# A decay projection in two waves, and the last block's inverse split between GpSimd and VectorE, in a linear-attention and expert kernel

## The chip, the cores and the metric

The kernel runs on one core of one Trainium2 chip. The metric is the device time of one execution in microseconds.

## The reference

One layer in float32 over x of 8 sequences, 512 steps, 256 channels (16 heads of 16). The first half mixes each step with the one before, makes r, k, v, a decay w, a removal direction kk with a strength a, and runs a state of 16x16 per head through the steps:

```python
w2 = jnp.tanh(xwa @ decay_w1.T) @ decay_w2
w = -jax.nn.softplus(-(time_decay + w2)) - 0.5
kk = k + jnp.tanh(xk @ kkk_w1.T) @ kkk_w2        # then divided by its norm per head
a = jax.nn.sigmoid(time_aaaaa + xwa @ aaa_w1.T @ aaa_w2)
...
def step(s, inp):
    q_, w_, k_, v_, a_, b_ = inp                 # w_ = exp(-exp(w)), a_ = kk, b_ = -kk * a
    sa = jnp.einsum('bhij,bhj->bhi', s, a_)
    s = s * w_[:, :, None, :] + sa[..., None] * b_[:, :, None, :] + v_[..., None] * k_[:, :, None, :]
    return (s, jnp.einsum('bhij,bhj->bhi', s, q_))
```

The outputs are normed per head, a bonus of r, k and v is added, and they are gated, projected by Wo, added to x and layer-normed. The second half sends each of the 4,096 tokens to one of 8 experts (the largest of 8 logits), norms it, and applies W1 (256 to 1,024), relu, W2 (back to 256), the residual and a last layer norm.

## The kernel before, in words

The 512 steps are cut in 16 blocks of 32 (`TB`). Within a block the recurrence is solved as a triangular system: `scores` makes the products of keys, removals and reads for all pairs of steps of a head; the part of it that belongs to removals is a 32x32 matrix for each of the 128 pairs of sequence and head, and its inverse is made on GpSimd (`invert`), one matrix per partition, column by column: for s from 30 down to 1 a product of s rows and 31-s columns (L1911) and its addition (L1914), 60 dependent operations. The scores go there over HBM by SP (`scores_to_pairs`: four stores to scr_n at L478, one load of `Up` at L483) and the inverse comes back the same way (`inverse_to_heads`: store to scr_u at L491, tokens of x at L460, four loads at L502). PE then multiplies by it (`solve`, in two parts, L718).

The blocks are staggered over the passes of one loop, `body(n)`, n from -2 to 18, written out for each engine in program order. In body n the projections and scores are those of block n+1, keys and values of block n are turned, block n-1 is solved, read out and its state updated, block n-2 is gated and projected by Wo, and block n-3 has its router logits taken. Nothing is scheduled by a planner: the order of calls in each engine's `body` is the order of its queue.

PE's results lie in six PSUM banks that a `Ring` gives out in a fixed order. An entry such as `k@3` means bank 3; a job may start once the reader of the job before it in the same bank has run (`freed` says which step that is), and `wait_empty` waits for that. In the stretch around the change PE runs `hidden` (L610), `gates`, `square` for k (both L576), the turn of some keys (L670), then `decay_a_kk` and `ma_mk` through `from_hidden` (L622: z with all 128 rows of the hidden vector, then a beside kk and ma beside mk, each with 32 rows), `router` and `project_out` (L576), `solve` part one (L718), `norms` (L576), `solve` part two, `square` for r and v, turns, `read_out` (L752), `bonus` (L576), `update` (L740) and `scores` (L662).

ScalarE (from `keep_z`) takes z with its bias, its sigma into the bank (L1058), a, ma, the absolute value (L1064), the logits of block n-3 (L1212), the square of kk (L1097), then after a table load (L1035) the logarithm (L1117), the norms (L1121), and the decays. VectorE, after the mixing for the next blocks, adds k to kk in `sum_kk` (L1420), runs the scan over sigma (L1400) in `sum_decays`, `key_gain` (L1406, L1408), `add_tokens` of block n-2 (L1546), which frees the bank that `norms` takes, `gain_keys` (L1424), the token statistics, `key_exponent` (L1412, L1414), `keep_x` (L1511), `normed_kk` (L1461), `decay_reads` (L1452), `decay_kk` (L1483), `removal` (L1467), `decay_keys` (L1429), `bonus_terms` (L1434), `mask_removal` (L1476) and `mask_keys` (L1445), for which `scores` waits. All these lines record operations for 128 partitions of 512 columns.

The last block is 15 (`last`). When its scores are done, no projections are left to fill the time of its inverse. W2 (8 MB, one DMA of 1 MB per expert, L513) is loaded over the arrays of the loop by `load_experts`, the first four experts in body 15 and the others in body 16.

## Time and profile before

| | |
|---|---|
| median of 3 runs | 1071.95 us (1068.2 to 1084.34) |
| profiled execution | 1076.19 us, span of its instructions 1074.1 us, mean granted TensorE clock 0.951 |
| PE / DVE / ACT / POOL busy | 980.1 / 768.0 / 519.9 / 613.1 us |
| blocks' loop | to about 660 us of the span |
| last inverse and routing | about 660 to 767 us |
| experts | 767 to 1,064 us |

Times within the span count from its start. The page names engines PE (TensorE), DVE (VectorE), ACT (ScalarE), POOL (GpSimd) and SP (SyncE). A row of the timeline merges instructions of the same kind that follow each other. Matmul times are modelled at their ends, so their sums run a little over the time that they take.

### The profile page before, as it was taken

How to read it: one execution, taken by the hardware profiler on the slowest of the kernel's cores; microseconds unless marked ns; L12 is line 12 of the kernel's file. 1: busy time of each engine (PE TensorE's matmuls, PEld its weight loads, DVE VectorE, ACT ScalarE, POOL GpSimd, SP SyncE). 2: the span in 40 equal slices, each digit the busy share in tenths (PEclk: the TensorE clock that was granted, in tenths of full speed). 3: DMA queues.
4: the chain of work that ended last, by engine and by line, in shares of the span. 5: the costliest groups of instructions: out<-in, count | busy, mean ns of one | idle time of the engine just before them, and what ended most of it. 6: DMA issues, size and time to landing. Idle time of an engine off the chain costs nothing.

```text
span 1074.1 us, 42156 instructions
## 1 busy us (share of the span) xinstructions
PE 980.1 (91%) x16652; PEld 801.8 (75%) x16653; DVE 768.0 (71%) x1793; ACT 519.9 (48%) x1081; POOL 613.1 (57%) x1135
## 2 busy tenths in 40 slices
PE   8898989999999989999999998679899999999995
PEld 5676777777777767777777776557899898989894
DVE  5766788889879778887688885266476666666663
ACT  4474576677677576676476783221122121212120
POOL 1088786788886787785867876810133333333321
PEclk9997999999999999998799998689999999999998
DMA  5113225225324225224143133746545445544430
GB/s 121 40 21 81 71 33 110 65 51 111 77 47 101 70 44 111 72 42 107 17 101 87 28 91 85 206 115 232 217 163 176 161 174 162 176 158 170 158 119 4
DMA packets 208894, 112.14 MB, mean 104 GB/s; under 512 B 172508, under 2 KB 192224, under 8 KB 208352
## 3 DMA queue, kind: packets, MB, share of 16 engines
q1 hardware_dynamic: 202352, 100.92, 35.0%
q0 software_dynamic: 3744, 8.40, 2.3%
q8 instruction: 121, 1.98, 0.8%
q10 hardware_dynamic: 2640, 0.54, 0.3%
q14 instruction: 37, 0.30, 0.1%
HBM read 85.57 MB, written 26.08 MB: 104 GB/s over the span
## 4 chain that ended last, share of the span: by engine, by line
PE 61%; DVE 14%; issue 8%; POOL 6%; DMA 5%; ACT 4%; DVEq 1%; SPq 1%; ACTq 0%; POOLq 0%
PE bank L576 16%; PE bank L970 12%; PE bank L983 9%; PE bank L662 6%; PE ry L983 4%; PE bank L718 3%; POOL arena L1914 3%; POOL arena L1911 3%; DVE bank L1389 2%; PE ry L692 2%; PE bank L594 1%; PE bank L622 1%; PE bank L950 1%; PE ry L698 1%; PE bank L740 1%
## 5 line engine op out<-in xcount | busy, mean ns | idle before, releaser
L576 PE MATMUL bank<-arena 128*128 128x256 f32 (+2 forms) x992 | 280.9, 422 | 22.4 <-DVE arena L1434 9.5
L1914 POOL TENSOR_TENSOR arena<-arena 128x30 f32<-128x30 f32 (+14 forms) x480 | 261.6, 545 | 37.6
L1911 POOL TENSOR_TENSOR arena<-arena 128x30 f32<-128x30 f32 (+14 forms) x480 | 250.5, 522 | 36.4
L576 PEld LDWEIGHTS bank<-arena 128*128 128x128 f32 x992 | 178.5, 203 | 67.9 <-issue 31.5
L970 PEld LDWEIGHTS bank<-arena 128*128 128x128 f32 x1248 | 146.8, 194 | 5.8 <-issue 3.0
L970 PE MATMUL bank<-arena 128*128 128x128 f32 x1248 | 147.5, 277 | 3.1 <-DVE arena L1820 2.5
L1498 DVE TENSOR_TENSOR arena<-bank,arena 128x512 f32<-128x512 f32 x128 | 79.5, 684 | 53.1 <-PE bank L662 53.1
L1302 ACT ACTIVATE arena<-arena 128x1 f32<-128x1 f32 x39 | 11.5, 294 | 178.6 <-DVE arena L1774 178.6
L983 PE MATMUL bank<-arena 128*128 x416 | 96.4, 385 | 0.1
L1945 POOL COPY arena<-arena 128x1 int32 (+1 forms) x39 | 7.1, 183 | 146.4 <-DVE arena L1838 146.4
L983 PEld LDWEIGHTS bank<-arena 128*128 128x128 f32 x416 | 76.9, 190 | 14.5 <-issue 4.9
L662 PE MATMUL bank<-arena 32*128 32x64 f32 x2048 | 68.9, 276 | 10.6 <-issue 6.4
L1939 POOL DMA_INDIRECT arena<-scr_x,arena x39 | 41.2, 1056 | 62.4 <-DVE arena L1756 31.4
L662 PEld LDWEIGHTS bank<-arena 32*128 32x128 f32 x2048 | 64.0, 189 | 14.9 <-issue 13.4
L1389 DVE SCALAR_TENSOR_TENSOR bank<-bank,arena 128x256 f32<-128x256 f32 x128 | 56.1, 484 | 22.2 <-PE bank L594 22.2
L670 PE MATMUL bank<-arena 128*128 128x128 f32 x432 | 62.5, 279 | 4.2 <-DVE arena L1511 1.6
L670 PEld LDWEIGHTS bank<-arena 128*128 128x128 f32 x432 | 52.1, 144 | 18.8 <-issue 12.4
L1904 POOL MEMSET arena<- 128x32 f32 x16 | 2.5, 157 | 111.2 <-DMA arena<-scr_n 111.2
L718 PEld LDWEIGHTS bank<-arena 32*64 32x64 f32 x2048 | 40.1, 157 | 34.6 <-issue 29.6
L1820 DVE TENSOR_SCALAR arena<-bank,arena 128x128 f32<-128x128 f32 x156 | 43.9, 345 | 24.6 <-issue 19.9
L1947 POOL DMA_INDIRECT out_dram<-arena x39 | 39.8, 1021 | 34.9 <-DVE arena L1804 20.8
L718 PE MATMUL bank<-arena 32*64 32x32 f32 x2048 | 43.8, 239 | 15.1 <-DMA arena<-scr_u 13.9
(173 smaller groups left out, 1757.7 us busy)
## 6 DMA issues: line engine op xcount, KB each, us to landing
arena<-in_W SPq DMA_DIRECT2D x47, 1024.0 KB, 5.1
scr_n<-arena SPq DMA_DIRECT2D x64, 128.0 KB, 3.0
arena<-scr_n SPq DMA_DIRECT2D x16, 512.0 KB, 3.7
scr_u<-arena SPq DMA_DIRECT2D x16, 512.0 KB, 4.5
arena<-scr_u SPq DMA_DIRECT2D x62, 128.0 KB, 2.9
arena<-in_xTp SPq DMA_DIRECT2D x32, 132.0 KB, 4.0
arena<-in_x SPq DMA_DIRECT2D x64, 64.0 KB, 2.7
scr_x<-arena SPq DMA_DIRECT2D x64, 64.0 KB, 1.8
```

Source lines behind the costliest of these rows:

```text
L576: mm = pe.matmul(ring.tile(m, name)[0:rows, to], lhsT, rhs, start=(i == 0), stop=(i == len(terms) - 1))
L662: mm = pe.matmul(ring.tile(m, f"sc{f}{p}")[:, b * 2 * TB:(b + 1) * 2 * TB], bkm[r, f * B + b, :], aq[m % 2][r, f * B + b].rearrange("p x t ...
L670: mm = pe.transpose(ring.tile(m, name)[:, i * P:(i + 1) * P], src, ident)
L718: mm[bank] = pe.matmul(ring.tile(m, f"x{bank}")[x_rows_of(e), at:at + 32], Ux[m % 2][r, g % 4, g // 4, e].rearrange("p h t -> p (h t)"), R ...
L970: mm = pe.matmul(hidT_ps[t // 4][:, (t % 4) * P:(t % 4 + 1) * P], W1[s][:, k, t * P:(t + 1) * P], xnT[:, k, :], start=(k == 0), stop=(k == ...
L983: mm = pe.matmul(y_ps[s][:, 0:D], hidT[s][:, t, :], W2f[:, bass.ds(e * (FT * D) + t * D, D)], start=(t == 0), stop=(t == FT - 1))
L1389: xm_ok.inc(m, f"{g}{h}", STT(out=part, in0=part, scalar=prm(f"maa{g}", h), in1=dx[:, h], op0=ALU.add, op1=ALU.mult))
L1498: score.inc(m, name, TT(sc[m % 2][:, f, p].rearrange("p k e x t -> p (k e) (x t)"), ring.tile(m, name)[:, :].rearrange("p (b n) -> p b n", ...
L1820: relu_dve.inc(str(t), nc.vector.tensor_scalar(hidT[s][:, t], hidT_ps[1][:, (t - 4) * P:(t - 3) * P], b1f[:, bass.ds(e * FT + t, 1)], 0.0, ...
L1911: inv_ok.inc(f"m{s}", TT(t, U[:, 0:s, s:s + 1].broadcast_to(shape), U[:, s:s + 1, s + 1:TB].broadcast_to(shape), ALU.mult))
L1914: inv_ok.inc(f"a{s}", TT(U[:, 0:s, s + 1:TB], U[:, 0:s, s + 1:TB], t, ALU.add))
L1939: nc.gpsimd.indirect_dma_start(out=xg[:, s], out_offset=None, in_=x_rows, in_offset=bass.IndirectOffsetOnAxis(ap=index, axis=0), bounds_ch ...
```

## The change

In the loop:

- z is made in two halves of 32 hidden rows. The first goes with a and kk (three matmuls side by side on the array, L639 to L642 of the changed kernel), the second, after `router`, with ma and mk (L653 to L656). z stays in its bank between them.
- kk is accumulated by PE onto k in bank 3. `sum_kk` of VectorE is gone; ScalarE copies the sum (`keep_kk`) and squares it from the bank.
- banks change: logits 3 to 0, xa 1 to 5, the turn of keys bk11 5 to 1, routing ranks 5 to 2. `square` for k comes before `gates`.
- ScalarE's order is a, logits, kk copy, square, z, sigma, ma, absolute value; the decay of keys and the growths come before the copy of bk11.
- VectorE's `decay_reads` comes after `bonus_terms`.
- ss, yc and var are filled in two matmuls of 256 columns instead of one of 512.

At the end:

- the last inverse is split at column 24 (`CUT`): GpSimd does the left 24x24, VectorE the right 8 columns in PSUM bank 2, with a copy of the left coefficients made by ScalarE (`keep_coefs`). VectorE's steps stand in three parts in body 15.
- the store of inverse 14 goes out before the load of matrix 15, and both halves of W2 are loaded in body 16, behind the last heads' reads.

```diff
-        ring = Ring(banks, [(0, "bk00@5"), (1, "h@2"), (-2, "g@4"), (1, "k@3"), (0, "bk01@2"), (1, "z@1 a@5 kk@3 ma@4 mk@2"),
-                            (-3, "logit@3"), (-2, "wo@0"), (1, "ss@0"), (-1, "xa@1 xb@3"), (1, "r@4"),
-                            (0, "bk11@5"), (1, "v@2"), (0, "bk10@5 v0@1 v1@3"),
+        ring = Ring(banks, [(0, "bk00@5"), (1, "h@2"), (1, "k@3"), (-2, "g@4"), (0, "bk01@2"), (1, "a@5 kk@3"), (-3, "logit@0"),
+                            (1, "z@1 ma@4 mk@2"), (-2, "wo@0"), (1, "ss@0"), (-1, "xa@5 xb@3"), (1, "r@4"),
+                            (0, "bk11@1"), (1, "v@2"), (0, "bk10@5 v0@1 v1@3"),
...
             def body(n):
-                if has(n - 1):
-                    inverse_to_heads(n - 1)
+                if has(n - 1) and n != last:
+                    store_inverse(n - 1)
+                    heads_from_inverse(n - 1)
...
-                if n == last:
+                if n == last + 1:
                     load_experts(slice(0, 4))
-                if n == last + 1:
                     load_experts(slice(4, E))
...
             def decay_a_kk(m):
                 hid_act.wait(pe, m, "decay", "copy", "kkk")
-                from_hidden(m, [[("z", 2, slice(0, P), hid)]])
-                from_hidden(m, [[("a", 0, slice(64, 96), hid), ("kk", 0, slice(96, 128), kkh)]])
+                for name in ("z", "a", "kk"):
+                    ring.wait_empty(pe, m, name)
+                for h, to in both:
+                    mm_z = pe.matmul(ring.tile(m, "z")[:, to], w_out[0:32, 2, hs(h)], hid[0:32, :], start=(h == 0), stop=False,
+                                     skip_group_check=True)
+                    mm_a = pe.matmul(ring.tile(m, "a")[:, to], w_out[64:96, 0, hs(h)], hid[64:96, :], start=True, stop=True)
+                    mm_kk = pe.matmul(ring.tile(m, "kk")[:, to], w_out[96:128, 0, hs(h)], kkh[96:128, :], start=False, stop=True,
+                                      skip_group_check=True)
...
-                fill(m, "ss", [(all_cols, [(head_sum, flat(nrm))])])
+                fill(m, "ss", [(to, [(head_sum, nrm[:, h])]) for h, to in both])
...
+            def keep_kk(m):
+                if m:
+                    comb.wait(act, m - 1, "kkn")
+                ring.wait_full(act, m, "kk")
+                proj.inc(m, "kk", A(flat(kk), bank(m, "kk"), ACT.Copy))
...
-            def sum_kk(m):
-                ring.wait_full(dve, m, "kk")
-                proj.wait(dve, m, "k")
-                comb.inc(m, "kk", TT(flat(kk), ring.tile(m, "kk")[:, :], flat(kt), ALU.add))
...
+            def invert_right(m, steps):
+                U = Up[m % 2]
+                for s in steps:
+                    last_inv_dve.wait(dve, 0, "start" if s == TB - 2 else f"a{s + 1}")
+                    c = max(s + 1, CUT) - CUT
+                    n = TB - CUT - c
+                    shape = [P, s, n]
+                    t = flat(L)[:, 0:s * n].rearrange("p (r c) -> p r c", r=s)
+                    column = U[:, 0:s, s:s + 1] if s >= CUT else coefs[:, 0:s, s:s + 1]
+                    last_inv_dve.inc(f"m{s}", TT(t, right[:, s:s + 1, c:].broadcast_to(shape), column.broadcast_to(shape), ALU.mult))
+                    last_inv_dve.wait(dve, 0, f"m{s}")
+                    last_inv_dve.inc(f"a{s}", TT(right[:, 0:s, c:], right[:, 0:s, c:], t, ALU.add))
...
+                if n == last:
+                    start_right(last)
+                    invert_right(last, range(TB - 2, 23, -1))
                 if has(n - 1):
                     keep_x(n - 1, "a", 0)
                     keep_x(n - 1, "a", 1)
                     keep_x(n - 1, "b", 1)
+                if n == last:
+                    invert_right(last, range(23, 12, -1))
...
+                if n == last:
+                    invert_right(last, range(12, 0, -1))
+                    keep_right(last)
...
+            for m in range(NBLK - 1):
                 invert(m)
+            invert_left(last)
```

How the rows move. First ScalarE in one body of the loop, before: the copy of k (L1085), one of keys (L1150), z (L1029 from bank 1), its sigma (L1058), a (bank 5), ma (bank 4), absolute value, logits, square, sigma of it, mk, table load, logarithm.

```order
L1085 ACTIVATE arena<-bank3 128x512
L1150 ACTIVATE arena<-bank2 128x512
L1029 ACTIVATE arena<-bank1,arena 128x256 x2
L1058 ACTIVATE bank1<-arena 128x512
L1029 ACTIVATE arena<-bank5,arena 128x256 x2
L1029 ACTIVATE bank4<-bank4,arena 128x256 x2
L1064 ACTIVATE arena<-arena 128x512
L1212 ACTIVATE arena<-bank3 128x16
L1097 ACTIVATE arena<-arena 128x512
L1068 ACTIVATE arena<-arena 128x512
L1029 ACTIVATE bank2<-bank2,arena 128x256 x2
L1035 ACT_TABLE_LOAD
```

The same place of the changed kernel (L1112 is the copy of k, L1182 of keys, L1244 the logits, L1129 the new copy of kk, L1123 its square, L1085 the sigma of z):

```order
L1112 ACTIVATE arena<-bank3 128x512
L1182 ACTIVATE arena<-bank2 128x512
L1056 ACTIVATE arena<-bank5,arena 128x256 x2
L1244 ACTIVATE arena<-bank0 128x16
L1129 ACTIVATE arena<-bank3 128x512
L1123 ACTIVATE arena<-bank3 128x512
L1056 ACTIVATE arena<-bank1,arena 128x256 x2
L1085 ACTIVATE bank1<-arena 128x512
L1056 ACTIVATE bank4<-bank4,arena 128x256 x2
L1091 ACTIVATE arena<-arena 128x512
L1095 ACTIVATE arena<-arena 128x512
```

z and its sigma moved behind a, the logits, the copy of kk and its square.

PE after the turn of keys, changed kernel, with the semaphores that each waits for (L639 z, L641 a, L642 kk; L595 `router` and then `project_out`; L653 z, L655 ma, L656 mk; L745 `solve`; the second L595 of 128x256 is `norms`, whose wait `tok` is `add_tokens`):

```order
L642 MATMUL bank<-arena 128x256
L595 MATMUL bank<-arena 128x8 [waits xm_ok,late_act]
L595 MATMUL bank<-arena 128x8 x3
L653 MATMUL bank<-arena 128x256 [waits turned,post_dve,half_decay]
L655 MATMUL bank<-arena 128x256
L656 MATMUL bank<-arena 128x256
L653 MATMUL bank<-arena 128x256
L655 MATMUL bank<-arena 128x256
L656 MATMUL bank<-arena 128x256
L595 MATMUL bank<-arena 128x256 [waits late_act,post_dve]
L595 MATMUL bank<-arena 128x256 x3
L745 MATMUL bank<-arena 64x32 [waits chain_dve,u_in,proj]
```

Before, `router` followed all of L622 and waited for `comb` (`sum_kk`), and now it stands between the waves and waits for `xm_ok` and `late_act`.

SP at the end of the loop, changed kernel (L507 store of an inverse, L468 tokens, L521 heads' reads, L532 W2, L476 stores of x1, L566 the rows of the layer norm):

```order
L476 DMA scr_x<-arena 32x2x256 x4
L468 DMA arena<-in_x 32x2x256 x4
L476 DMA scr_x<-arena 32x2x256 x4
L507 DMA scr_u<-arena 128x1024
L468 DMA arena<-in_x 32x2x256 x4
L521 DMA arena<-scr_u 32x32x32 x2
L532 DMA arena<-in_W 128x8x256 x8
L476 DMA scr_x<-arena 32x2x256 x8
```

Before, four of the eight loads of W2 stood between the first two rows.

## Rows read from the trace of the kernel before

**Rows 1.** The page, busy time of each engine

```profile
PE 980.1 (91%) x16652; PEld 801.8 (75%) x16653; DVE 768.0 (71%) x1793; ACT 519.9 (48%) x1081; POOL 613.1 (57%) x1135
```

**Rows 2.** Timeline of PE: start, us, instructions [idle before <-releaser]

```profile
330.46 1.07 PE L610 MATMUL bank<-arena 128*32 128x256 f32 x16
...
334.59 2.96 PE L622 MATMUL bank<-arena 128*128 128x256 f32 x20
338.23 2.86 PE L576 MATMUL bank<-arena 128*128 128x8 f32 x16 [0.69 <-DVE arena L1420]
341.02 1.13 PE L718 MATMUL bank<-arena 32*64 32x32 f32 x64
...
351.17 1.10 PE L576 MATMUL bank<-arena 128*128 128x256 f32 x4 [0.80 <-DVE arena L1434]
...
354.03 0.73 PE L662 MATMUL bank<-arena 32*128 32x64 f32 x17
...
371.39 0.85 PE L610 MATMUL bank<-arena 128*32 128x256 f32 x12
...
500.57 2.96 PE L622 MATMUL bank<-arena 128*128 128x256 f32 x20
```

**Rows 3.** Timeline of DVE, the same two bodies

```profile
338.01 1.20 DVE L1400 TENSOR_TENSOR_SCAN arena<-arena,bank 128x512 f32<-128x512 f32 x1
339.13 0.66 DVE L1406 SCALAR_TENSOR_TENSOR arena<-bank,arena 128x512 f32<-128x512 f32 x1
339.83 0.70 DVE L1408 TENSOR_TENSOR bank<-bank,arena 128x512 f32<-128x512 f32 x1
341.20 0.69 DVE L1546 TENSOR_TENSOR arena<-bank,arena 128x512 f32<-128x512 f32 x1 [0.67 <-PE bank L576]
...
352.13 1.75 DVE L1445 TENSOR_TENSOR arena<-arena 128x512 f32<-128x512 f32 x2
...
523.35 1.68 DVE L1445 TENSOR_TENSOR arena<-arena 128x512 f32<-128x512 f32 x2
```

**Rows 4.** Waits over the whole span: us in total, times, longest

```profile
PE bank L576 <- DVE arena L1434: 9.5, 13, 1.4
DVE arena L1546 <- PE bank L576: 14.8, 13, 2.8
```

**Rows 5.** Timeline of POOL, the last inverse

```profile
668.13 0.25 POOL L1911 TENSOR_TENSOR arena<-arena 128x30 f32<-128x30 f32 x1
...
684.91 0.64 POOL L1914 TENSOR_TENSOR arena<-arena 128x240 f32<-128x240 f32 x1
...
702.62 0.27 POOL L1914 TENSOR_TENSOR arena<-arena 128x30 f32<-128x30 f32 x1
```

**Rows 6.** Timeline of SP, its DMA issues

```profile
674.74 6.18 SPq L513 DMA_DIRECT2D arena<-in_W  x4
```

**Rows 7.** Timeline of PE, after the loop

```profile
674.83 3.94 PE L718 MATMUL bank<-arena 32*64 32x32 f32 x128 [6.25 <-DMA arena<-scr_u]
...
689.77 0.38 PE L752 MATMUL ry<-arena 128*32 128x32 f32 x11 [4.70 <-issue]
...
710.15 3.94 PE L718 MATMUL bank<-arena 32*64 32x32 f32 x128 [4.13 <-DMA arena<-scr_u]
```

**Rows 8.** Timeline of ACT, the first body above

```profile
335.72 0.84 ACT L1029 ACTIVATE arena<-bank,arena 128x256 f32<-128x256 f32 x2 [0.22 <-PE bank L622]
336.59 0.60 ACT L1058 ACTIVATE bank<-arena 128x512 f32<-128x512 f32 x1
...
342.53 0.63 ACT L1117 ACTIVATE arena<-arena 128x512 f32<-128x512 f32 x1
```

**Rows 9.** Timeline of DVE, small operations in a chain

```profile
702.36 0.43 DVE L1573 TENSOR_TENSOR arena<-arena 128x224 f32<-128x224 f32 x1
...
737.14 0.19 DVE L1573 TENSOR_TENSOR arena<-arena 128x32 f32<-128x32 f32 x1
```

**Rows 10.** Busy time in a stretch, the granted clock third from the end

```profile
504.00:512.00 8.00, 8.00 (x82) 6.01 (x82) 5.09 (x12) 5.01 (x10) 7.03 (x13) 0.53 0.59 99
```

More of the change, by code:

```diff
@@ L612, in hidden @@
                 ring.fill(m, "h", mm)
-            def from_hidden(m, parts):
-                for group in parts:
-                    for name, w, rows, x in group:
-                        ring.wait_empty(pe, m, name)
-                for group in parts:
-                    for h, to in both:
-                        for name, w, rows, x in group:
-                            mm = pe.matmul(ring.tile(m, name)[:, to], w_out[rows, w, hs(h)], x[rows, :], start=True, stop=True)
-                            if h == HALF - 1:
-                                ring.fill(m, name, mm)
@@ L1263, in body @@
                     growths(n + 1)
+                if has(n) and n < last:
+                    keep_keys(n, 1, 1)
                 if has(n) and n < last:
```

129 lines of the change are left out of this document (94 added, 35 removed).

## The prediction

> **What bounds the kernel now.** I read the page first: PE is busy 91% of the span, DVE 71% [rows 1]. That would make it a PE kernel, in which every matmul removed is time gained. So I next read one body of the main loop in order of time, engine by engine. The body that starts with `hidden` at 330.46 us ends with the next `hidden` at 371.39, 40.9 us later; the loop has 16 such bodies and they fill the span up to about 660 us. PE waits twice in it for VectorE: 0.69 us ahead of `router`, for `sum_kk` (L1420), and 0.80 us ahead of `bonus`, for L1434 [rows 2]. Where does VectorE's time come from? It waits 0.67 us for `project_out` before `add_tokens` (L1546, 341.20), and from there it works almost without a gap to the end of `mask_keys` (L1445), at 352.13 + 1.75 = 353.88; `scores` (L662) starts on PE at 354.03, 0.15 us later [rows 2, 3]. So the cycle has two parts: PE alone from `scores` to the hidden outputs (L622, 334.59), and then a chain that goes over PE to `add_tokens` and down VectorE to `scores`. I count times in a body from the start p of L622: `add_tokens` starts at p+6.61, `mask_keys` ends at p+19.29.
>
> The groups of waits say that this is the rule: L1546 waited 13 times for PE, 14.8 us in all; PE waited 13 times for L1434, 9.5 us [rows 4]. After the loop the bound is another: the last inverse on GpSimd, from 668.1 to 702.62 + 0.27 = 702.89 us, its store and the reads of it, and `solve` at 710.15 [rows 5, 6, 7]. From 767 us the experts run on PE, and the change leaves them alone.
>
> **The loop, part by part.** Taken from PE: the two full matmuls of z. L622 is z, a/kk and ma/mk, 20 records in 2.96 us [rows 2]; the matmuls of a pair stand in other rows of the array and run side by side, so the group is two single matmuls and four pairs, six slots of about 0.45 us with the fill and drain. Now it is two waves of three side by side, four slots: about 2.0 us, 0.9 us less. With the wait of 0.69 before `router` gone (its bank no longer waits for `sum_kk`), `project_out` ends about 1.6 us earlier, at p+4.9 instead of p+6.5. If nothing else bound, `add_tokens` could start there.
>
> It can't, because z now comes with the second wave and last on ScalarE. Before, ScalarE takes z first, at 335.72 = p+1.13, and its sigma (L1058) starts at 336.59 and ends at p+2.60 [rows 8]. Now: a at p+1.2 (0.72 to the next), the logits wait for `router` (wave one 1.07 + router 1.03, and 0.1 to the reader): p+2.15; the new copy of kk at p+2.25; the square 0.50 later, p+2.75; z another 0.50 later, p+3.25 (the second wave is there at p+3.2); sigma 0.87 later, p+4.12, ended p+4.75. VectorE's scan stands behind it: p+4.8 instead of 338.01 = p+3.42. The scan, the two operations of `key_gain` and `add_tokens` follow at 1.12, 0.70 and 0.77 us, spacings read off [rows 3]: `add_tokens` at p+7.39, 0.78 us later than now, though PE's result has lain there for 2.4 us. `sum_kk`'s 0.68 us that VectorE saves is lost in the idle time ahead of the scan. A second path gives the same: ScalarE has one more operation (the kk copy, 0.60), so its logarithm (L1117), at p+7.94 now [rows 8], starts near p+8.7 and ends p+9.35, and L1412, at p+8.76 now [rows 3], can't start before p+9.4; by the first path it starts at p+9.54.
>
> From `add_tokens` to the end of `mask_keys` VectorE has the same work as before, 12.68 us, with one difference: the read of r with the decay moves behind `bonus_terms`. It used to stand between an operation and its follower; without it the follower waits for its own input. The pair L1483 to L1467, which waits so, is 0.78 us apart, the others 0.60: 0.17 us more. So `mask_keys` ends at p+20.24 against p+19.29, 0.95 us later, and `scores` with it. PE gets a new wait: `norms` needs the bank that `add_tokens` frees, at about p+8.2, while `solve`'s first part ends at p+5.95: some 2.2 us idle, with the second part of `solve`, r, v and the turns queued behind. The wait ahead of `bonus` shrinks to about 0.4, and one of 0.7 appears ahead of `scores`. Splitting ss, yc and var in halves adds weight loads that run beside matmuls: 0, with bounds of 0.1 us on either side per fill.
>
> That is a body at the full clock. In others `project_out` itself is late, and the early PE helps. L1546's mean wait is 14.8/13 = 1.14 us against 0.67 in the body above [rows 4], so the mean body has `add_tokens` near p+7.0 and gains a delay of 0.4, with the 0.17 some 0.6 us. Thirteen bodies: +7.5. The three first ones, with no `add_tokens`, hang on the logarithm: +0.8 each, +2.4. Sum of the loop **+10 us**. Bounds: PE alone, below; and +1.4 for every body, if all were full-clock ones with `project_out` on time, +20.
>
> **The last inverse.** GpSimd keeps 24 columns: 44 instructions over 4,048 elements. One takes 0.25 us at 30 elements and 0.64 at 240 [rows 5], and the next starts 0.08 later, so 0.28 + 1.8 ns per element: 19.6 us instead of 34.8. VectorE takes 8 columns, with 60 instructions over 5,872 elements and two copies. Its dependent small operations take 0.19 us at 32 elements and 0.43 at 224 [rows 9], with the next 0.03 or less behind, so about 0.19 + 1.05 ns per element: 4.2 us for the first 7 steps, 7.5 for 11, 5.9 for 12, and 0.9 of copies. But they stand in VectorE's queue between other work. The matrix arrives about when it does now (its load shares the DMA with the store of inverse 14, which goes ahead of it instead of after it): 667.5. Statistics of block 13 to 669, first part to 674; `keep_x` of block 14 waits for `solve`, which comes some 4 us earlier since inverse 14 is stored earlier (now `solve` idles 6.25 us for it [rows 7]), 676.6; 11 steps to 684; state and tokens to 686.4; 12 steps and the copy to 692.7. VectorE ends last, 10.2 us before GpSimd does now. Ahead of `solve` PE has `gates`, `project_out` and `rank_known`, behind VectorE's `choose_known`: they end near 700, with the heads.
>
> From this goes what W2 costs. Its first half, 4 MB, was issued at 674.74 and filled the DMA while nothing waited, except that PE stood 4.70 us for "issue" at 685 to 689.77, off the path [rows 6, 7]. Now all 8 MB go out right behind the heads, beside the last `solve` and `read_out`, which stand on the path. Bounds: 0, and the same 4.7 us; I take 2, since fewer instructions follow than there. The experts need the first of W2 after 767, long after. Gain **-8 us**, from -12 (no stall, VectorE's steps closely packed) to 0.
>
> **Sum.** The profiled execution took 1076.19 us (span 1074.1), 4.2 above the median of 1071.95. +10 - 8 = +2: 1078 by that execution. I take off 4 for the median, and add 1 for the clock (below): **1075 us**.
>
> **The clock, and a rule of the skill.** PE's granted clock is at 1.2 GHz in stretches: from 504 to 512 us the mean is 0.53 of full [rows 10], after a body whose L622 began at 500.57; that body's `mask_keys` ends at 523.35 + 1.68 = p+24.46, 5.2 us later than in the body above [rows 2, 3]. Ahead of the fall stood L622, a wait of under 1 us and the small `router`. The changed body has a wait of 2.2 us between the small matmuls of `solve` and `norms`. The Trainium skill (TensorE: Matmul & The Clock Gate, HAM oscillation) says that short bursts between waits send the array back to half rate again and again. The trace's falls, near waits of a microsecond, go with it.
>
> **The rivals.** *PE sets the pace.* If sigma and the scan are not on the path as I count (z taken earlier, or VectorE with slack), each of 13 bodies gets the 0.9 of z and the two waits, 0.69 and 0.80: 2.4 us, -31 together; with -8 at the end 1072 - 39 = 1033. For it: PE's 91%. Against it: VectorE's unbroken 12.7 us up to `scores`. *The clock falls in every new wait.* One stretch at half rate of 3.5 us costs 1.75 on PE, of which the 1.1 of waits ahead of `bonus` and `scores` hides most; but a long one as at 504 costs 5.2. From 4 such bodies in 13 the total passes the 2%; with 5, 26 us: 1075 + 26 = 1101, slower. For it: the row at 504; against it: r and v, full-size matmuls, come right after and should bring the rate back. *The last inverse gains nothing*, because VectorE's part is queued longer or W2 meets the last heads' reads: 1075 + 8 = 1083, no change that can be told.
>
> **The numbers.** Forecast 0.62, PE sets the pace 0.13, the clock 0.17, no gain at the end 0.08. A measurement of this kernel tells about 2% from no change: 1050.5 and 1093.4. Faster: 0.13 and 0.01 of the forecast; slower: the clock's 0.17 and 0.01; the same: 0.68. Range: 1046 to 1096, from the near edge of the first rival to that of the second.
>
> **What would show it.** Right: a wait of the scan for ScalarE of 1 to 2 us and of `norms` for `add_tokens` of about 2 in each body; none of `router` for VectorE; `mask_keys` ending near p+20.2; VectorE's last copy some 5 us behind GpSimd's last step, `solve` 8 us earlier counted from the last `scores`; PE waiting for "issue" beside W2. Wrong: bodies of 39 us or less with `add_tokens` before p+6, or the clock at half after each `solve`.

## The result, and the profile after

The changed kernel takes 1109.8 us (median of 4 runs, 1103.7 to 1115.8) beside 1074.9 (1068.2 to 1084.3) for the kernel before on the same chip: a ratio of 1.034, with a 95% interval of 1.029 to 1.039. It is slower. Forecast were 1075 and no measurable change; the result lies outside the range. Here and below the ratios, and not the medians, leave out executions in a slower state that some fall into: of the four of `e1_tail` they leave 1083.0 and 1068.3, too few for a ratio, and the profile of `e15_z_first_fill` is of a slow one.

The profiled execution took 1109.02 us, of which the span is 1107.2 (before: 1076.19 and 1074.1, so +33.1 in the span). Line numbers below are those of the changed kernel: L639 with L641, L642 is the first wave and L653, L655, L656 the second (both were L622), L595 all filled banks (L576), L689 `scores` (L662), L1482 `mask_keys` (L1445), L1607 `add_tokens` (L1546), L745 `solve` (L718), L779 `read_out` (L752). Columns are as in the rows of before.

Span and mean granted TensorE clock after:

```profile
core 0: 1107.2 us, clock 0.928
```

Two of PE's lines after. Behind the last bar stand its idle time in us and then what ended most of it, each with its own us:

```profile
L595 PE MATMUL bank<-arena 128*128 128x256 f32 (+1 forms) x1088 | 301.5, 420 | 34.5 <-DVE arena L1607 20.6 <-DVE arena L1461 3.6 <-DVE arena L1591 3.5
L689 PE MATMUL bank<-arena 32*128 32x64 f32 x2048 | 68.0, 274 | 12.4 <-ACT arena L1193 8.6 <-issue 3.2 <-DVE arena L1535 0.3
```

The wait for VectorE's `add_tokens` (20.6 us) is the one of `norms` that was counted. Before, these fills waited 9.5 us for L1434 [rows 4]. The other was not counted: `scores` now waits 8.6 us for L1193, ScalarE's `keep_values`, in 9 bodies. Before, the same wait was 2.4 us in 4 bodies, a row that the prediction did not look at; from the list of waits of before (us, times, longest):

```profile
PE bank L662 <- ACT arena L1161: 2.4, 4, 1.1
```

One body in order of time, PE, VectorE and ScalarE; it answers to [rows 2, 3, 8]:

```profile
349.95 0.48 PE L639 MATMUL bank<-arena 32*128 32x256 f32 x1
...
355.00 1.13 PE L745 MATMUL bank<-arena 32*64 32x32 f32 x64
358.08 1.10 PE L595 MATMUL bank<-arena 128*128 128x256 f32 x4 [1.94 <-DVE arena L1607]
...
360.28 3.52 PE L595 MATMUL bank<-arena 128*128 128x256 f32 x8
...
365.80 1.47 PE L697 MATMUL bank<-arena 128*128 128x128 f32 x12
...
371.27 2.01 PE L689 MATMUL bank<-arena 32*128 32x64 f32 x64 [0.94 <-ACT arena L1193]
```

```profile
354.81 1.22 DVE L1442 TENSOR_TENSOR_SCAN arena<-arena,bank 128x512 f32<-128x512 f32 x1 [2.19 <-ACT bank L1085]
...
357.25 0.68 DVE L1607 TENSOR_TENSOR arena<-bank,arena 128x512 f32<-128x512 f32 x1
...
368.61 1.74 DVE L1482 TENSOR_TENSOR arena<-arena 128x512 f32<-128x512 f32 x2
```

```profile
354.11 0.60 ACT L1085 ACTIVATE bank<-arena 128x512 f32<-128x512 f32 x1
...
366.50 0.60 ACT L1182 ACTIVATE arena<-bank 128x512 f32<-128x512 f32 x1 [1.57 <-PE bank L697]
367.00 1.20 ACT L1193 ACTIVATE arena<-bank 64x512 f32<-64x512 f32 x2
...
369.85 1.20 ACT L1193 ACTIVATE arena<-bank 64x512 f32<-64x512 f32 x2
```

With p = 349.95, sigma ends at p+4.76 (counted 4.75), `add_tokens` starts at p+7.30 (7.39), `mask_keys` ends at 370.35 = p+20.40 (20.24). The steps counted are there. But `scores` starts at p+21.32, not with `mask_keys`: ScalarE's last copy of the turned values ends at 371.05, and two of the banks of `scores` are those that it reads. The row of before that answers to it ends at 353.66, just ahead of `mask_keys` at 353.88 [rows 3]:

```profile
352.45 1.21 ACT L1161 ACTIVATE arena<-bank 64x512 f32<-64x512 f32 x2
```

ScalarE is late now because it waited 1.57 us for PE's turned keys (L697). Why PE turned them late shows beside the same rows of before, `norms`, the fills of r and the last turns:

```profile
342.08 1.13 PE L576 MATMUL bank<-arena 128*128 128x512 f32 x2
...
344.20 1.99 PE L576 MATMUL bank<-arena 128*128 128x256 f32 x8
...
348.20 1.47 PE L670 MATMUL bank<-arena 128*128 128x128 f32 x12
```

`norms` starts at p+7.49 before and at p+8.13 after, 0.64 us later: PE reached it earlier and then stood 1.94 us. The last turns start at p+13.61 and p+15.85, 2.24 later. The other 1.60 us lie between the two and are the slower clock: the eight fills of r take 3.52 us in place of 1.99. So the wait of `norms`, which I took for one with slack behind it, comes back through the clock and ScalarE.

The clock, in the stretch from `norms` to the turns, after and then before (granted clock third from the end):

```profile
359.00:367.00 8.00, 8.00 (x96) 6.88 (x96) 7.52 (x15) 5.78 (x12) 7.22 (x11) 0.79 0.01 2
```

```profile
342.00:350.00 8.00, 8.00 (x154) 6.48 (x150) 7.75 (x16) 7.01 (x13) 7.14 (x12) 1.00 0.20 28
```

Some 2 us behind the end of the wait of 1.94 us the clock falls to 1.2 GHz for 3.4 us; before, it stays at 2.4 GHz. In the twelve bodies of the table below ten have 6.8 us or more at half rate, before one has.

The end, after. The last steps of the inverse on GpSimd and VectorE:

```profile
719.99 0.22 POOL L1999 TENSOR_TENSOR arena<-arena 128x22 f32<-128x22 f32 x1
```

```profile
724.99 0.42 DVE L1574 COPY arena<-bank 128x256 f32<-128x256 f32 x1
```

VectorE ends 5.2 us behind GpSimd, as counted (5). Then the inverse's store, W2's loads, and PE (see [rows 5 to 7]):

```profile
725.48 0.34 SPq L507 DMA_DIRECT2D scr_u<-arena  x1
...
728.52 0.92 SPq L521 DMA_DIRECT2D arena<-scr_u  x2
729.54 24.75 SPq L532 DMA_DIRECT2D arena<-in_W  x8
```

```profile
734.85 2.10 PE L745 MATMUL bank<-arena 32*64 32x32 f32 x110 [0.68 <-DMA arena<-scr_u]
741.22 0.84 PE L745 MATMUL bank<-arena 32*64 32x32 f32 x18 [4.27 <-issue]
...
747.62 0.53 PE L779 MATMUL ry<-arena 128*32 128x32 f32 x19 [1.83 <-issue]
```

Where the 33.1 us are: up to VectorE's last read of scores, 658.63 before and 689.94 after, **+31.3**. From there to `solve` of the last block 51.5 before and 44.9 after, **-6.6**. Then to the end of the last `read_out` 8.1 and 13.3, **+5.2**, with both "issue" rows in it. The rest, 355.8 and 359.1, **+3.2**: the prediction left this part alone, and no run takes it apart. It is 357.0 to 359.2 us in the changed kernel and the ten made from it, and 355.3 to 358.0 in the kernel before and the six made from it.

### The profile page after: what moved, and what is told of

It is laid out like the page before. It is cut to its first block, busy times and chain, and to the rows that moved or that the text cites. A ratio compares the mean times of both kernels' runs of the same rounds, so it can differ in the third digit from the quotient of the medians.

```text
span 1107.2 us, 42510 instructions
## 1 busy us (share of the span) xinstructions
PE 991.3 (90%) x16812; PEld 828.1 (75%) x16813; DVE 776.0 (70%) x1839; ACT 534.1 (48%) x1098; POOL 597.5 (54%) x1119
## 4 chain that ended last, share of the span: by engine, by line
PE 56%; DVE 14%; issue 8%; ACT 6%; POOL 6%; DMA 5%; DVEq 2%; SPq 1%; ACTq 0%; POOLq 0%
PE bank L595 18%; PE bank L1010 9%; PE bank L997 6%; PE bank L689 5%; PE bank L697 3%; POOL arena L1981 3%; POOL arena L1978 3%; PE bank L745 3%; PE ry L719 2%; DMA scr_u<-arena 2%; PE ry L725 1%; DMA arena<-scr_u 1%; DVEq L1827 1%; PE ry L1010 1%; PE bank L614 1%
## 5 line engine op out<-in xcount | busy, mean ns | idle before, releaser
L595 PE MATMUL bank<-arena 128*128 128x256 f32 (+1 forms) x1088 | 301.5, 420 | 34.5 <-DVE arena L1607 20.6
L595 PEld LDWEIGHTS bank<-arena 128*128 128x128 f32 x1088 | 211.3, 214 | 90.6 <-issue 32.2
L1981 POOL TENSOR_TENSOR arena<-arena 128x30 f32<-128x30 f32 (+14 forms) x450 | 243.8, 542 | 35.3
L1978 POOL TENSOR_TENSOR arena<-arena 128x30 f32<-128x30 f32 (+14 forms) x450 | 236.6, 526 | 34.1
L997 PEld LDWEIGHTS bank<-arena 128*128 128x128 f32 x1248 | 146.8, 194 | 6.1 <-issue 3.3
L997 PE MATMUL bank<-arena 128*128 128x128 f32 x1248 | 147.5, 277 | 3.5 <-DVE arena L1887 2.8
L1010 PEld LDWEIGHTS bank<-arena 128*128 128x128 f32 x416 | 76.9, 190 | 14.4 <-issue 4.8
L689 PE MATMUL bank<-arena 32*128 32x64 f32 x2048 | 68.0, 274 | 12.4 <-ACT arena L1193 8.6
L689 PEld LDWEIGHTS bank<-arena 32*128 32x128 f32 x2048 | 63.1, 187 | 16.6 <-issue 14.5
L745 PEld LDWEIGHTS bank<-arena 32*64 32x64 f32 x2048 | 44.3, 170 | 33.1 <-issue 18.2
L697 PE MATMUL bank<-arena 128*128 128x128 f32 x432 | 65.2, 287 | 3.3 <-DVE arena L1548 1.2
L745 PE MATMUL bank<-arena 32*64 32x32 f32 x2048 | 48.2, 250 | 20.0 <-DMA arena<-scr_u 13.4
L697 PEld LDWEIGHTS bank<-arena 128*128 128x128 f32 x432 | 54.0, 148 | 14.9 <-issue 7.4
L1182 ACT ACTIVATE arena<-bank 128x512 f32<-128x512 f32 x60 | 35.8, 597 | 48.8 <-PE bank L697 48.4
```

Of the source, the lines that this page charges most:

```text
L595: mm = pe.matmul(ring.tile(m, name)[0:rows, to], lhsT, rhs, start=(i == 0 and not (started_once and j)), stop=(i == len(terms) - 1), skip_ ...
L689: mm = pe.matmul(ring.tile(m, f"sc{f}{p}")[:, b * 2 * TB:(b + 1) * 2 * TB], bkm[r, f * B + b, :], aq[m % 2][r, f * B + b].rearrange("p x t ...
L697: mm = pe.transpose(ring.tile(m, name)[:, i * P:(i + 1) * P], src, ident)
L745: mm[bank] = pe.matmul(ring.tile(m, f"x{bank}")[x_rows_of(e), at:at + 32], Ux[m % 2][r, g % 4, g // 4, e].rearrange("p h t -> p (h t)"), R ...
L997: mm = pe.matmul(hidT_ps[t // 4][:, (t % 4) * P:(t % 4 + 1) * P], W1[s][:, k, t * P:(t + 1) * P], xnT[:, k, :], start=(k == 0), stop=(k == ...
L1010: mm = pe.matmul(y_ps[s][:, 0:D], hidT[s][:, t, :], W2f[:, bass.ds(e * (FT * D) + t * D, D)], start=(t == 0), stop=(t == FT - 1))
```

## The experiments

For each kernel the table gives, from its one profiled execution, the twelve bodies from the fourth `hidden` to the sixteenth, in sums of us: from `hidden` to the end of `mask_keys`, from there to the first `scores`, from `scores` to the next `hidden`, and the time in these bodies at half rate (half-microsecond windows with their granted clock). Then the time from the last read of scores to the last `solve`, and from that to the end of the last `read_out`. The median and the ratio are of all timed executions.

```
kernel            to mask_keys  to scores  to hidden   sum   half rate | to solve  read_out | median  ratio [95%]
before                   291.7        6.0      194.6  492.3     37.6   |   51.5       8.1   |
after                    308.4       17.9      193.2  519.5     92.2   |   44.9      13.3   | 1109.8  1.034 [1.029, 1.039]
e1_tail                  297.1       10.2      192.3  499.5     44.3   |   51.5       8.1   | 1083.7
e2_loop                  302.1       14.1      196.2  512.4     78.5   |   51.5      10.6   | 1107.5  1.027 [1.018, 1.036]
e3_fill                  298.2       14.3      197.9  510.4     17.0   |   46.7      11.0   | 1103.3  1.024 [1.017, 1.032]
e4_tokens_first          302.9        7.1      205.4  515.5     51.2   |   48.4      10.7   | 1103.9  1.024 [1.017, 1.032]
e5_fill_norms            300.0        3.6      199.3  502.9     27.3   |   54.6       8.1   | 1097.8  1.026 [1.014, 1.037]
e6_w2_late               306.2       19.3      195.8  521.4     88.8   |   42.1      10.4   | 1099.8  1.025 [1.015, 1.036]
e7_router                300.7       10.6      199.9  511.2     61.4   |   52.7      12.5   | 1110.5  1.037 [1.025, 1.049]
e8_before_tail           289.6        7.8      197.8  495.2     47.8   |   46.7       5.9   | 1069.1  0.997 [0.992, 1.002]
e9_z_first               298.8        9.7      197.3  505.8     58.1   |   45.7       8.0   | 1086.2  1.005 [1.001, 1.010]
e10_q_early              304.9       13.4      192.4  510.7     78.4   |   43.5      13.0   | 1114.2  1.034 [1.027, 1.041]
e11_before_fill          289.1        7.4      202.2  498.7     37.5   |   45.0       7.0   | 1067.1  0.988 [0.980, 0.997]
e12_before_waves         298.3        5.8      197.8  501.9     44.4   |   51.5       7.4   | 1088.1  1.012 [1.002, 1.021]
e13_combined             308.1       13.0      197.6  518.7     68.3   |   44.4       5.9   | 1089.0  1.013 [1.006, 1.021]
e14_z_first_q            286.8        5.7      198.5  491.0     27.3   |   45.8       6.5   | 1074.2  0.999 [0.995, 1.004]
e15_z_first_fill         294.7       10.4      199.4  504.6     41.0   |   47.5       6.5   | 1083.4  1.009 [1.005, 1.013]
e16_again                291.1        4.4      198.2  493.7     30.7   |   42.7       6.5   | 1070.3  0.999 [0.994, 1.003]
```

The kernel before ran from 1062.8 to 1090.3 us beside these, and the untouched loop of before took 492.3, 499.5 and 495.2 us in three profiles, so differences of some 7 us between single profiles say nothing. The experiments ran on four chips, so ratios compare better than medians. Of the 27.2 us that the twelve bodies lost, 16.7 are in the first column, 11.9 in the second and none in the third (-1.4).

### Which half: e1_tail, e2_loop

`e1_tail` is the kernel before with the split inverse and W2 behind it; `e2_loop` the changed kernel without them.

```
 e2_loop, last block:
-    for m in range(NBLK - 1): invert(m)
-    invert_left(last)
+    for m in range(NBLK): invert(m)
```

> The kernel before with the last inverse split between GpSimd and VectorE, and W2 loaded behind it, alone; the loop is that of before. My forecast gave this part -8 us, so 1067. What the two traces show since is that the split brings solve(15) 6.6 us nearer to the last scores, that the last solves and read-outs take 5.2 us longer beside W2's loads, and that the rest behind them is 3.2 us longer: sum +1.8, so 1077 (1071 to 1082), with an end (last scores read by VectorE to the end of the last read_out) within 3 us of before's 59.6 us.

> The changed kernel with the last inverse back on GpSimd alone and W2 at its old two places: only the loop is changed. If the whole loss lies in the loop, as the two traces say (+31.3 us up to the last scores), this takes 1106 (1100 to 1112), and the half-rate time in the loop stays near 90 us. If the split and the loop harm each other, it lies below 1095. My forecast of the loop's part was +10, so 1085.

The loop alone costs nearly all: 1107.5. The tail alone does not gain the 8 us of the forecast: its four executions run from 1068.3 to 1087.6 beside 1068.7 to 1083.3, so whether it loses can't be told. Its trace says where the gain went. The issues of SP and ScalarE, and PE:

```profile
700.67 0.34 SPq L506 DMA_DIRECT2D scr_u<-arena  x1
...
704.49 26.46 SPq L531 DMA_DIRECT2D arena<-in_W  x8
```

```profile
705.35 0.96 ACTq L1239 DMA_DIRECT2D arena<-scr_u  x2
```

```profile
716.96 3.94 PE L736 MATMUL bank<-arena 32*64 32x32 f32 x128 [6.19 <-DMA arena<-scr_u]
```

```profile
712.00:716.00 4.00, 0.00 (x0) 0.00 (x0) 0.00 (x0) 0.00 (x0) 0.00 (x0) 1.00 1.15 324
```

The last read of scores was at 665.48, so the inverse is stored 35.2 us behind it, against 702.91 - 658.63 = 44.3 before: the split itself gave 9.1 (6.4 to 11.1 over the fifteen kernels that have it). But from the store to `solve` it took 16.3 us in place of 7.2, with every engine idle at its end and the DMA engines full of W2 (share 1.15). The whole gain went there. The price goes with when ScalarE issues its two of the four loads of the heads, behind its copy of the logits. In `e1_tail` it came at 705.35, behind the first load of W2 at 704.49, and so it was in e5 and e7 (17.2 and 16.6 us). In the changed kernel, e3 and e9 ScalarE issued before W2, and the stretch took 9.4, 8.8 and 8.0 us. No run moves these two loads alone.

### The end: e6_w2_late, e8_before_tail

```
 load_experts(some):
-    if some.stop == E:
+    if some.stop:
         ring.wait_full(sp, last, "v0", "v1")
         chain_pe.wait(sp, last, "Y")
```

> The changed kernel with all eight W2 loads held until the last read_out is done. Theory: W2's packets delay the last inverse's way to the heads and stall the last solves and read-outs. Then solve(15) starts 42 to 43 us behind the last scores (44.9 in the changed kernel), the stretch from it to the last read_out takes 8.1 us (13.3), and the time is 1102 (1098 to 1106). If the stalls of 4.27 and 1.83 us in that stretch don't come from W2's loads, they stay, and the time is 1108 to 1111.

> The kernel before with the split of the last inverse and all of W2 behind the last read_out. In e1_tail the inverse was stored 9.1 us earlier behind the last scores, but solve(15) came no earlier (+51.5 us both times), with W2's loads at 0.9 to 1.1 of the DMA share beside the heads' loads. Theory (W2 took the gain): solve(15) comes at +42.5, 8 to 10 us are gained, 1066 (1060 to 1070). Rival (the store and the loads of the heads are slow for another reason): +50 or more, 1072 to 1078.

With W2 behind the last `read_out`, `solve` comes at +42.1 in the changed kernel, 9.4 earlier than before the change (counted: 10.2 without W2). The median falls from 1109.8 to 1099.8, but the intervals of the two ratios overlap, and the two stretches of the table are shorter by 5.7 us together, so the 10 is in part luck. In the loop of before `solve` comes at +46.7, and the time is 1069.1, level with the kernel before. Half of the split's gain is still missing there; PE in e8_before_tail:

```profile
696.56 7.16 PE L594 MATMUL bank<-arena 128*128 128x256 f32 x20 [2.57 <-DVE arena L1580]
...
706.15 2.35 PE L736 MATMUL bank<-arena 32*64 32x32 f32 x128
```

```profile
697.00:703.00 6.00, 6.00 (x19) 5.09 (x19) 2.92 (x8) 0.18 (x1) 0.00 (x0) 0.50 0.76 148
```

The inverse was stored at 695.14, and by the 7.2 us of before the heads would be there at about 702.3, an estimate. But VectorE, busy with its share of the inverse, normed an earlier block late (L1580); PE waited 2.57 us for it and then did the fills ahead of `solve` at 1.2 GHz, up to 706.15. My reading of the "issue" rows was half right. In e6_w2_late PE's stall in `read_out` stands where it stood, with no W2 load under way:

```profile
746.55 0.53 PE L779 MATMUL ry<-arena 128*32 128x32 f32 x19 [1.83 <-issue]
```

The one in `solve` shrank from 4.27 to 1.36. So 1.83 us are not W2's. The stretch from `solve` to the end of `read_out` took 10.4 us where 8.1 was expected, and the time fell within its range all the same.

### Waits or the clock: e3_fill, e5_fill_norms, e11_before_fill, e16_again

```
 body(n), e5_fill_norms:
     solve(n - 1, 0)
+    keep_busy(3, ring.tile(n - 1, "xa")[:, 2 * P:4 * P])
 scores(m, 0), e3_fill besides:
+    ring.wait_empty(pe, m, "sc00")
+    keep_busy(2, ring.tile(m, "sc00"))
```

> The changed kernel with three unused 256-column matmuls ahead of norms and two ahead of the first scores, in every body; all waits of the other engines stay as they are. Theory A (the clock: the two waits per body let it fall to half rate, and half-rate matmuls are the larger part of the loss): half-rate time in the loop falls from 92 to 60 us or less and the time to 1085 to 1100. Theory B (the waits are the loss; the clock only goes along with them): the clock rises but the time stays within 5 us of 1110, or grows, since a filler that outlasts its wait delays what is behind it.

> The changed kernel with the three unused matmuls ahead of norms alone, none ahead of the scores. In e3_fill the two fillers ahead of the scores ended up to 1 us behind mask_keys in most bodies and so cost what they saved. If the clock is a large part of the loss, this takes 1088 to 1097, with the time from mask_keys to the first scores under 6 us in bodies 3 to 14 (17.9 in the changed kernel, 14.3 with both fillers) and half-rate time under 45 us. If the clock hardly matters, 1103 to 1110.

Unused matmuls make the kernel faster. With three ahead of `norms` nothing else is removed or moved, yet the twelve bodies fall from 519.5 to 502.9 us and the median from 1109.8 to 1097.8. The ratios, 1.034 and 1.026, have intervals that overlap; the direction rests on the traces and on both kernels with fillers: of their eight executions five lie below the changed kernel's lowest, 1103.7, and none above its second lowest, 1109.0. Mean clocks of e3_fill and e5_fill_norms:

```profile
core 0: 1099.7 us, clock 0.970
```

```profile
core 0: 1093.4 us, clock 0.961
```

With the filled wait the turned keys come in time, and the wait of `scores` for ScalarE is gone; its line in e5_fill_norms:

```profile
L689 PE MATMUL bank<-arena 32*128 32x64 f32 x2048 | 70.1, 277 | 11.1 <-issue 8.0 <-DVE arena L1483 3.0
```

That was theory A of e3_fill, though its time, 1103.3, stayed above the 1085 to 1100 expected: the clock rose by 0.042, and two fillers ahead of `scores` ended behind `mask_keys` and cost again (14.3 us against 3.6). So the half rate is worth about 12 to 17 of the 31 us in the loop, an estimate from e5_fill_norms; the rest is lateness at full rate. The Trainium skill (TensorE: Matmul & The Clock Gate, HAM oscillation) describes bursts of matmuls that fall back to half rate in every wait between them, in a kernel whose waits are longer than these. The runs here show it behind waits of some 2 us, with 92 us at half rate in twelve bodies and 27 with fillers.

Would fillers help the loop of before? One ahead of `project_out`, one ahead of `bonus`:

> The kernel of e8_before_tail (the loop of before, the split inverse, W2 behind the last read_out) with one unused matmul ahead of project_out and one ahead of bonus in every body, where TensorE waits 0.7 and 0.8 us. Theory (short waits cost the clock in the loop of before too): half-rate time in bodies 3 to 14 falls from 48 us to under 25 and 5 to 10 us are gained on e8_before_tail: 1061. Rival (the half-rate time there starts at stalls within the scores, which no filler covers): 1067 to 1072.

> The kernel of e11_before_fill again, in more rounds: whether it beats the kernel before. If its 0.988 was real, 0.985 to 0.995 with an interval below 1; if it was the luck of four runs, 0.995 to 1.003.

Four runs said 0.988 [0.980, 0.997], twelve more of the same kernel on another chip 0.999 [0.994, 1.003]: the first was most likely luck. No version here beats the kernel before by what can be told.

### Which edit of the loop: e4, e7, e9, e10, e12, e14

`e4_tokens_first` puts `add_tokens` ahead of the scan on VectorE.

> The changed kernel with add_tokens ahead of the scan and key_gain on VectorE. Theory A (the wait of norms for add_tokens, 20.6 us on the page, delays the turned keys by some 2 us, so ScalarE's copies of the turned values end late, and the scores wait for those): norms waits under 5 us in all, the wait of scores for ScalarE falls from 8.6 to 4 or less, 1095 to 1103. Theory B (VectorE's chain sets the body): the scan starts 0.4 us later per body and mask_keys ends as much later, 1112 to 1118.

As theory A says, `scores` waits for ScalarE falls to 2.4 us, but it takes 1103.9, just above the 1095 to 1103 expected, and the gain of 6 us is not clear of noise: the intervals of the two ratios overlap. VectorE and PE now wait elsewhere, from the list of waits of e4_tokens_first:

```profile
DVE arena L1607 <- PE bank L595: 40.7, 15, 4.1
PE bank L595 <- DVE arena L1489: 21.8, 12, 2.3
```

L1489 is `decay_reads`: it frees the bank of `bonus`, and since the change moves it behind `bonus_terms`, it ends late. A wait was traded for another.

`e7_router` puts the router's matmuls behind the second wave.

> The changed kernel with the router's matmuls (1.0 us) behind the second wave of the projections in place of between the waves, its bank and copy moved to match: z is full 1.0 us earlier in every body, and nothing else is changed. Theory (sigma's late end is the first cause; all waits follow from it): sigma ends 8.0 us behind the body's start in place of 8.98, norms waits 1.0 in place of 1.94 us, mask_keys ends 0.7 to 1.0 earlier, half-rate time falls too, and the time is 1088 to 1098. Rival (VectorE or ScalarE set the body by their own work): under 5 us gained, 1105 to 1110.

z is full 1 us earlier, but sigma ends only 0.32 us earlier, since ScalarE has the kk copy and the square ahead of z, in e7_router:

```profile
357.10 0.60 ACT L1129 ACTIVATE arena<-bank 128x512 f32<-128x512 f32 x1
357.57 0.61 ACT L1123 ACTIVATE arena<-bank 128x512 f32<-128x512 f32 x1
358.05 0.86 ACT L1056 ACTIVATE arena<-bank,arena 128x256 f32<-128x256 f32 x2
358.94 0.60 ACT L1085 ACTIVATE bank<-arena 128x512 f32<-128x512 f32 x1
```

And the router, in its moved bank, now waits 0.9 us for the square. Some 8 us (519.5 to 511.2) came in the twelve bodies, about the size of the noise, and as much was lost at the end, where `solve` came at +52.7 beside W2: 1110.5, a miss against 1088 to 1098.

`e9_z_first` undoes the waves and with them ScalarE's order, and nothing else:

```
-    order on PE:       z(0:32) + a + kk | router | z(32:64) + ma + mk
-    order on ScalarE:  a, logits, kk, square, z, sigma
+    order on PE:       z (128 rows) | a + kk | router | ma + mk
+    order on ScalarE:  z, sigma, a, logits, kk, square
```

> The changed kernel with the decay projection whole and first again (two matmuls of 128 rows per half ahead of a and kk), and z's copy and sigma first on ScalarE, as in the kernel before; banks, kk in one bank with k, keys ahead of the gates, the late reads and the tail stay changed. Theory (the second wave holds up sigma, and that starts the waits): sigma ends 6.8 to 7.2 us behind the body's start in place of 8.98, norms waits under 0.5 us, mask_keys ends 23.2 to 23.8 behind it in place of 24.6, half-rate time in bodies 3 to 14 goes from 92 to 40 us, and the time is 1080 (1072 to 1090) although TensorE computes 1.3 us more per body. Rival (banks, the kk copy and the late reads cost the time, not the waves): 1100 to 1110.

This is the largest single effect: 1109.8 falls to 1086.2, and the ratio from 1.034 to 1.005 [1.001, 1.010], though PE computes more. How much of it is the wave on PE and how much z's late turn on ScalarE, this run does not part. Sigma ends 6.73 us behind `hidden` as before the change, and no `norms` waits for L1603, its `add_tokens`, longer than 0.2 us. `mask_keys` ends 23.9 to 24.5 us behind `hidden` in the six shortest of the twelve bodies, and at 23.1 to 23.7 in seven bodies of before.

`e10_q_early` and `e14_z_first_q` put `decay_reads` back; the latter on top of e9_z_first, with W2 late.

> The changed kernel with decay_reads behind normed_kk again, ahead of decay_kk, as in the kernel before. It is the last write that frees the bank of bonus, so bonus has waited for it (up to 1.4 us in bodies whose chain is early). mask_keys comes no earlier. Theory: bonus waits shorter, but the first scores wait for mask_keys and for ScalarE's copies all the same, so 1106 to 1112, within noise of the changed kernel. Rival (this wait is one of those that cost the clock): 1098 to 1104 and at least 15 us less half-rate time.

> e9_z_first with decay_reads at its old place and W2 behind the last read_out. e9_z_first was 0 to 10 us slower than the kernel before, with mask_keys ending 0.65 us later per body and bonus waiting 1.2 to 1.6 us for decay_reads. If the late decay_reads is the rest of the loop's loss, then 1066 to 1074 with the end's gain of some 8 us; if the kk copy on ScalarE is (ln starts 0.4 us later), bodies 3 to 14 keep over 500 us and the time is 1076 to 1084.

Alone it changes nothing that can be told (1114.2). With the waves undone the twelve bodies go from 505.8 to 491.0 us, level with before's 492.3. These 14.8 us are too many for it: by the ratios, 1.005 and 0.999, this and W2 moved late give some 6 us together, and the profile of e14_z_first_q (1068.4) is one of its fastest executions. VectorE's rows in e9_z_first, then in e14_z_first_q:

```profile
364.29 0.68 DVE L1494 SCALAR_TENSOR_TENSOR bank<-bank,arena 128x512 f32<-128x512 f32 x1
365.10 0.69 DVE L1516 TENSOR_TENSOR arena<-bank,arena 128x512 f32<-128x512 f32 x1
365.90 0.70 DVE L1500 SCALAR_TENSOR_TENSOR bank<-bank,arena 128x512 f32<-128x512 f32 x1
366.51 1.00 DVE L1462 TENSOR_TENSOR arena<-arena 128x512 f32<-128x512 f32 x1
```

```profile
313.64 0.68 DVE L1494 SCALAR_TENSOR_TENSOR bank<-bank,arena 128x512 f32<-128x512 f32 x1
314.24 0.67 DVE L1485 TENSOR_TENSOR arena<-bank,arena 128x512 f32<-128x512 f32 x1
314.83 0.67 DVE L1516 TENSOR_TENSOR arena<-bank,arena 128x512 f32<-128x512 f32 x1
315.61 0.70 DVE L1500 SCALAR_TENSOR_TENSOR bank<-bank,arena 128x512 f32<-128x512 f32 x1
316.22 0.77 DVE L1462 TENSOR_TENSOR arena<-arena 128x512 f32<-128x512 f32 x1
```

A follower of its own input starts 0.81 us behind it, another instruction 0.60. `decay_reads` (L1485) fills that gap. From L1494 to the end of `mask_keys` it is 7.42 us with `decay_reads` late and 7.00 with it early: 0.2 are the gap, and 0.23 the shorter `decay_keys` (L1462, 1.00 and 0.77). And `bonus` no longer waits for it so long. So kk in the bank of k, the copy on ScalarE, the keys ahead of the gates and the other banks together cost and gave nothing that these runs can tell.

`e12_before_waves` does the waves alone in the kernel before, router behind both.

> The kernel before with the decay projection in two waves and nothing else: the first half of z beside a and kk, the second beside ma and mk, and ScalarE's copy of a ahead of that of z; the router stays behind both waves, kk and k are still added on VectorE. TensorE computes 1.3 us less per body, sigma ends some 1 us later (near 7.8 us behind the body's start in place of 6.73), and in before's bodies VectorE starts the scan at 7.1 to 7.8 anyway. Theory from e9 and e7 (it is z behind the router and behind the kk copy and square that costs; waves alone cost only what sigma is late by): within 6 us of the kernel before, 1070 to 1082. Rival (the waves as such cost the 24 us that e9 gave back): 1092 or more, with half-rate time in bodies 3 to 14 over 60 us.

1088.1, ratio 1.012 [1.002, 1.021]: some 10 us, between theory and rival. Sigma ended 8.56 us behind `hidden`, 1.8 later than before and not 1 as expected. The waves seem to cost by themselves, even without the router between them, though the interval nearly reaches 1; in the changed kernel, behind the router, the copy and the square, 24.

The two attempts at a version that beats both kernels:

> e11_before_fill (loop of before, one filler ahead of project_out and of bonus, split inverse, W2 behind the last read_out) with the two waves of e12_before_waves. If the waves without the router between them are free or better, 1062 to 1068, as fast as e11_before_fill or faster; if later sigma costs by itself, 1072 to 1080.

> e14_z_first_q (the changed kernel with z whole and first, decay_reads at its old place, W2 behind the last read_out) with the one filler ahead of project_out and of bonus of e11_before_fill. If the fillers give what they gave there (some 5 us), 1065 to 1070, level with e11_before_fill. If they fill waits that this loop does not have, 1072 to 1080.

Neither does. Waves on top of e11_before_fill give 1089.0, some 19 us above the 1070.3 of twelve runs without them, though TensorE computes less; that is more than the 1072 to 1080 expected if late sigma costs by itself. The fillers on top of e14_z_first_q give 1083.4, ratio 1.009 [1.005, 1.013], outside both ranges expected (1065 to 1070, 1072 to 1080). That last result has no explanation here.

## Why the prediction was wrong

- **The body's bound**, a chain over sigma, VectorE and `scores`: right as far as it went. PE had less to compute and the body got longer; z first again is 24 us faster with more matmuls.
- **The steps in the body shown**: right to 0.16 us, up to `mask_keys`.
- **"The same work as before, 12.68 us"**, from `add_tokens` to the end of `mask_keys`, plus 0.17: the failing step. The delay of `add_tokens` in the mean body came as counted: it starts 11.28 us behind `hidden` before and 11.68 after, +0.40. But from there to the end of `mask_keys` the mean body takes 13.04 us before and 14.02 after, +0.98 in place of 0.17 (13.46 with the fillers of e5_fill_norms). I gave VectorE no wait on this stretch. It waits there for `solve`'s second part (3.0 us in the twelve bodies before, 8.5 after) and for the turned keys (none before, 3.1 after), and both stand on PE behind the wait of `norms`. I wrote that they queue there, and priced nothing for it. The row of the second wait, after (us, times, longest):

```profile
DVE arena L1513 <- PE bank L697: 3.5, 7, 1.0
```

- **"`scores` with it"**: false, the second failing step. `scores` needs banks that ScalarE's `keep_values` frees. In before's body above that ended 0.22 us ahead of `mask_keys` (353.66 to 353.88), a margin that I did not look for. It cost (17.9 - 6.0) / 12 = 1.0 us per body. e4 and e5 both bring the turned keys earlier, and their stretch to `scores` is 7.1 and 3.6 us.
- **The clock**, taken at +1 and as a rival at 0.17: it is the cause of a good part of both steps. The rival had five long falls of 5.2 us; the trace has a fall in nearly every body, of 7 to 14 us at half rate. My argument against it, that r and v come right behind the wait, fails: they are what runs at 1.2 GHz. Sum of the loop: +31.3 against +10, of which fillers take back 17 in the twelve bodies.
- **`decay_reads` moved, 0.17**: 0.4 us in one body at full clock, of which 0.2 are the gap counted, and in e4, e5 and e9 a new wait of `bonus` for it, where I had the wait shrinking.
- **The last inverse, -8**: the split gives 9.1 in e1_tail and 8.8 in the changed kernel, where 10.2 was counted. The W2 term (2 us, bounds 0 and 4.7) was the mis-sized one: I priced it as a stall of PE's instructions, and the larger loss is the heads' own transfer, some 2 us in the changed kernel and 9 to 10 where ScalarE's loads came behind W2's. Net up to the last `read_out`: -6.6 + 5.2 = -1.4 in the changed kernel and 0 in `e1_tail`. The +3.2 behind it was taken at nothing, and its cause stays open.
- **"PE sets the pace", 1033**: excluded by the result, and by e9_z_first, which gains with more matmuls.

## What to carry to other kernels

When a copy moves later, follow every buffer behind it, not only the longest chain: a second engine with 0.2 us of slack becomes the bound next. Price a new wait of about 2 us on TensorE, repeated in each body, by the clock as well as by its length, and try a few unused matmuls in it before blaming the wait. Do not issue a bulk load beside the small transfer that the path waits for, least of all where a second engine issues part of that transfer and may come late; a semaphore that holds the bulk load until the result is there cost nothing that these runs show (e8: 355.3 us from there to the end, 355.8 before).

## What the runs showed of the hardware that I had not expected

- Three unused matmuls per body, some 1.5 us of work, go with 12 us less (1109.8 to 1097.8).
- With ScalarE's two of the four small loads of the heads issued behind the first load of W2, `solve` starts 16.3 to 17.2 us behind the inverse's store (e1, e5, e7); with all four ahead of it 8.0 to 9.4 where PE waits for them (e3, e9, changed kernel); with no W2 beside them 7.2.
- `decay_keys` (one multiply, 128x512, all in SBUF) takes 932 ns in the mean with `decay_reads` late (e9_z_first) and 737 with it early (e14_z_first_q); it is 792 in the kernel before and 871 after. The work is the same; why it differs I did not test.
- PE stands 1.83 us for "issue" at the same matmul of the last `read_out` with and without W2's loads. What it is stays open.
